# Out-projection of sixteen-head attention as three f16 products of split operands, on one Trainium2 core

## The reference

```python
q = jnp.einsum('bsd,hde->bhse', x, Wq)      # likewise k, v
scores = jnp.einsum('bhse,bhte->bhst', q, k)  # causal, / sqrt(64)
attn = jax.nn.softmax(scores, axis=-1)
out = jnp.einsum('bhst,bhte->bhse', attn, v)
heads = out.transpose(0, 2, 1, 3).reshape(B, S, H * E)
y = x + heads @ Wo                          # the out-projection
```

## Time and profile before

| | us |
|---|---|
| runs, median (lowest to highest of 3) | 846.56 (846.43 to 847.8) |
| the profiled execution, whole time | 846.91 |
| its span in the trace | 845.0 |
| busy: TensorE / its weight loads | 736.2 / 527.8 |
| busy: VectorE / ScalarE / GpSimd | 629.1 / 561.1 / 516.2 |
| output projection L890, 64 pairs, matmuls busy | 68.4 |
| idle of GpSimd ahead of L1022, until VectorE's split | 203.3 |

### The profile page before, as it was taken

The page is one execution under the profiler, slowest core; times in us unless marked ns, Lnnn a source line. Parts: engine busy times, 40 slices in busy tenths (PEclk is TensorE's granted clock), DMA queues, the critical chain, the costliest instruction groups (busy, mean ns, idle before and its releaser), DMA issues. The chain is left out here.

```text
span 845.0 us, 20974 instructions
## 1 busy us (share of the span) xinstructions
PE 736.2 (87%) x7594; PEld 527.8 (62%) x7594; DVE 629.1 (74%) x1291; ACT 561.1 (66%) x1551; POOL 516.2 (61%) x496
## 2 busy tenths in 40 slices
PE   4887678636999999999999999999999999999752
PEld 3656566533667766766676667667767667676541
DVE  1577766653766688689879877997898699789963
ACT  1466656633767766777777777777777777776633
POOL 3566653531655677666857775785667568666821
PEclk9998888778999999999999999999999999999965
DMA  7500000000798887877778878977787877788720
GB/s 189 127 1 1 0 2 0 1 0 18 146 152 142 146 146 140 145 143 137 144 139 149 148 143 138 153 139 147 141 142 141 145 146 143 151 139 157 136 50 23
DMA packets 360614, 94.00 MB, mean 111 GB/s; under 512 B 347584, under 2 KB 360384, under 8 KB 360512
## 3 DMA queue, kind: packets, MB, share of 16 engines
q1 hardware_dynamic: 357248, 90.57, 59.3%
q10 hardware_dynamic: 3264, 2.10, 0.8%
HBM read 6.63 MB, written 2.10 MB: 10 GB/s over the span
## 5 line engine op out<-in xcount | busy, mean ns | idle before, releaser
L1022 POOL TENSOR_TENSOR prob_hl<-prob,prob_hl 128x768 f16<-128x768 f32 (+1 forms) x192 | 347.4, 1809 | 203.3 <-DVE prob_hl L962 203.1
L933 ACT ACTIVATE prob<-wide,neg_max 128x128 f32<-128x128 f32 (+3 forms) x512 | 264.1, 524 | 157.7 <-DVE neg_max L974 157.6
L974 DVE TENSOR_REDUCE neg_max<-wide 128x2 f32<-128x256 f32 (+3 forms) x256 | 204.6, 820 | 111.7 <-PE wide L851 110.8
L846 PE MATMUL wide<-k_sb,q_sb 64*128 64x128 f32 (+3 forms) x1024 | 190.1, 469 | 0.9 <-ACT k_sb L828 0.8
L962 DVE CAST prob_hl<-prob 128x768 f16<-128x768 f32 (+1 forms) x192 | 155.0, 807 | 0.6 <-ACT prob L933 0.5
L871 PE MATMUL bank<-v_hi,prob_t 128*128 128x64 f16 x1280 | 133.1, 194 | 13.8 <-DMA prob_t<-prob_hl 12.2
L873 PE MATMUL bank<-v_hi,prob_t 128*128 128x64 f16 x1280 | 133.2, 194 | 0.0
L872 PE MATMUL bank<-v_lo,prob_t 128*128 128x64 f16 x1280 | 133.1, 193 | 0.0
L871 PEld LDWEIGHTS bank<-v_hi,prob_t 128*128 128x128 f16 x1280 | 115.8, 98 | 20.6 <-issue 13.7
L873 PEld LDWEIGHTS bank<-v_hi,prob_t 128*128 128x128 f16 x1280 | 114.5, 98 | 0.0
L872 PEld LDWEIGHTS bank<-v_lo,prob_t 128*128 128x128 f16 x1280 | 114.4, 98 | 0.0
(11 more groups left out here) (169 smaller groups left out, 1329.7 us busy)
## 6 DMA issues: line engine op xcount, KB each, us to landing
prob_t<-prob_hl SPq DMA_TRANSPOSE x384, 2.8
x_sb<-in_L_attn_a_in_features SPq DMA_DIRECT2D x8, 256.0 KB, 6.0
out_x<-x_done SPq DMA_DIRECT2D x8, 256.0 KB, 2.5
wq_a<-in_L_attn_a_w_q ACTq DMA_DIRECT2D x1, 512.0 KB, 5.2
wk_a<-in_L_attn_a_w_k ACTq DMA_DIRECT2D x1, 512.0 KB, 6.8
wo_a<-in_L_attn_a_w_o ACTq DMA_DIRECT2D x1, 512.0 KB, 7.5
wv_a<-in_L_attn_a_w_v ACTq DMA_DIRECT2D x1, 512.0 KB, 8.1
wq_b<-in_L_attn_b_Wq SPq DMA_DIRECT2D x1, 512.0 KB, 9.7
```

What stands on the lines that cost most here:

```text
L846: pe.matmul(dst[:, h, c:c + m], q[e, i * P:(i + 1) * P], k[e, 0:m], start=(i == UNIT_ROWS[u][0]), stop=False)
L933: last = act.activation(prob_2[s][:, at:at + m], score_banks(p, s)[:, h, c:c + m], ACT.Exp, bias=neg_max[p % 2][:, h, i:i + 1], accum_out= ...
L974: last = dve.tensor_reduce(neg_max[p % 2][:, :, i:i + 1], score_banks(p, s)[:, :, c:c + m], AX.X, ALU.max, negate=True)
L1022: pool.tensor_tensor(prob_hl[u][:, w:2 * w], prob_2[u][:, 0:w], prob_hl[u][:, 0:w], ALU.subtract)\
```

## The change

The weights Wo are divided by their own mean maximum and split into `wo_hi` and `wo_lo`, both f16, where they were multiplied by the scale of Wv before and stayed f32. ScalarE copies the turned context out of PSUM twice, to f16 (`ctx_t_hi`) and to f32 (`ctx_t`), and GpSimd subtracts one from the other in SBUF (`ctx_t_lo`, f16). It does so behind the low half of unit 1, in stage 1 of its own loop. The out-projection is three f16 products for each block where it was one f32 product, and waits for `ctx_t_lo`. The product of both scales is applied when YA is added to the residual.

```diff
...
         wv_b_lo = sb("wv_b_lo", [P, O], F32R)
-        wo_up = sb("wo_up", [P, HP, P])
-        largest = sb("largest", [P, 1])
+        wo_hi = sb("wo_hi", [P, HP, P], F16)
+        wo_lo = sb("wo_lo", [P, HP, P], F16)
+        y_scale = sb("y_scale", [P, 1])
+        largest = sb("largest", [P, 2])
         mean_of_rows = sb("mean_of_rows", [P, P])
-        scale_up = sb("scale_up", [P, 1])
-        scale_down = sb("scale_down", [P, 1])
+        scale_up = sb("scale_up", [P, 2])
+        scale_down = sb("scale_down", [P, 2])
...
         ctx_t = sb("ctx_t", [P, S])
+        ctx_t_hi = sb("ctx_t_hi", [P, S], F16)
+        ctx_t_lo = sb("ctx_t_lo", [P, S], F16)
         ffn_s = sb("ffn_s", [P, S])
...
         def scale_tensor(pe):
-            pe.wait_ge(sem("largest"), 1)
+            pe.wait_ge(sem("largest"), 2)
             pe.wait_ge(sem("mean_of_rows"), 1)
             pe.wait_ge(sem("at_g"), B)
-            pe.matmul(GX[:, 0:1], mean_of_rows[:, :], largest[:, :], start=True, stop=True).then_inc(sem("scale_ps"), 1)
+            pe.matmul(GX[:, 0:2], mean_of_rows[:, :], largest[:, :], start=True, stop=True).then_inc(sem("scale_ps"), 1)
...
                 .then_inc(sem("largest"), 1)
+            dve.tensor_reduce(largest[:, 1:2], wo_b[:, :, :], AX.XY, ALU.max, apply_absolute_value=True)\
+                .then_inc(sem("largest"), 1)
...
             act.copy(wv_b_hi[:, :], wv_b[:, :, :]).then_inc(sem("wv_b_hi"), 1)
+            act.wait_ge(sem("wo_b_scaled"), 1)
+            act.copy(wo_hi[:, :, :], wo_b[:, :, :]).then_inc(sem("wo_hi"), 1)
...
             dve.wait_ge(sem("scale_ps"), 1)
-            dve.tensor_scalar_max(scale_up[:, :], GX[:, 0:1], TINY).then_inc(sem("scale_up"), 1)
+            dve.tensor_scalar_max(scale_up[:, :], GX[:, 0:2], TINY).then_inc(sem("scale_up"), 1)
             dve.wait_ge(sem("scale_up"), 1)
...
                 .then_inc(sem("wv_b_scaled"), 1)
-            dve.tensor_scalar(wo_up[:, :, :], wo_b[:, :, :], scale_up[:, 0:1], None, ALU.mult)\
-                .then_inc(sem("wo_up"), 1)
+            dve.tensor_scalar(wo_b[:, :, :], wo_b[:, :, :], scale_down[:, 1:2], None, ALU.mult)\
+                .then_inc(sem("wo_b_scaled"), 1)
+            dve.tensor_tensor(y_scale[:, :], scale_up[:, 0:1], scale_up[:, 1:2], ALU.mult).then_inc(sem("y_scale"), 1)
...
                               ALU.subtract).then_inc(sem("wv_b_lo"), 1)
+            dve.wait_ge(sem("wo_hi"), 1)
+            dve.wait_ge(sem("wo_b_scaled"), 1)
+            dve.tensor_tensor(wo_lo[:, :, :], wo_b[:, :, :], wo_hi[:, :, :], ALU.subtract).then_inc(sem("wo_parts"), 1)
...
             n = number(b, p)
-            wait(pe, "ctx_t", n + 1)
+            wait(pe, "ctx_t_lo", n + 1)
             if p == 0:
...
             for i in range(QB):
-                last = pe.matmul(YA[:, i * P:(i + 1) * P], ctx_t[:, i * P:(i + 1) * P], wo_up[:, p, :],
-                                 start=(p == 0 and i == 0), stop=(p == HP - 1 and i == QB - 1))
+                block = slice(i * P, (i + 1) * P)
+                pe.matmul(YA[:, block], ctx_t_hi[:, block], wo_hi[:, p, :], start=(p == 0 and i == 0), stop=False)
+                pe.matmul(YA[:, block], ctx_t_hi[:, block], wo_lo[:, p, :], start=False, stop=False)
+                last = pe.matmul(YA[:, block], ctx_t_lo[:, block], wo_hi[:, p, :], start=False,
+                                 stop=(p == HP - 1 and i == QB - 1))
             last.then_inc(sem("y_ps"), 1)
...
                     wait(act, "y_ps", n - 2)
+                    wait(act, "ctx_t_lo", n - 2)
+                    act.copy(ctx_t_hi[:, :], MB[:, :]).then_inc(sem("ctx_t_hi"), 1)
                     act.copy(ctx_t[:, :], MB[:, :]).then_inc(sem("ctx_t"), 1)
...
             n = number(b, p)
+
+            def context_lower(u):
+                if u == 1 and pair_exists(*earlier(b, p, 2)):
+                    wait(pool, "ctx_t_hi", n - 1)
+                    wait(pool, "ctx_t", n - 1)
+                    wait(pool, "y_ps", n - 2)
+                    pool.tensor_tensor(ctx_t_lo[:, :], ctx_t[:, :], ctx_t_hi[:, :], ALU.subtract)\
+                        .then_inc(sem("ctx_t_lo"), 1)
+
             if pair_exists(b, p):
...
                         .then_inc(sem(f"pl{u}"), 1)
+                    context_lower(u)
                     back_gpsimd(pool, b, p, u)
...
                 for u in range(NU):
+                    context_lower(u)
                     back_gpsimd(pool, b, p, u)
...
                     m = 2 * len(unit_blocks(u))
-                    sp.wait_ge(sem("wo_up"), 1)
+                    sp.wait_ge(sem("wo_parts"), 1)
                     wait(sp, f"ph{u}", n + 1)
...
                     sp.dma_start_transpose(prob_t[u][:, 0:m, :], prob_hl[u][:, 0:m * P]).then_inc(sem(f"pt_hi{u}"), 16)
-                    sp.wait_ge(sem("wo_up"), 1)
+                    sp.wait_ge(sem("wo_parts"), 1)
                     wait(sp, f"pl{u}", n + 1)
...
             tokens = y_res[:, seq(c), :]
-            dve.tensor_tensor(tokens, YA[:, :].rearrange("p (a d) -> p a d", d=P), tokens, ALU.add)\
+            wait(dve, "y_scale", 1)
+            dve.scalar_tensor_tensor(out=tokens, in0=YA[:, :].rearrange("p (a d) -> p a d", d=P),
+                                     scalar=y_scale[:, 0:1], in1=tokens, op0=ALU.mult, op1=ALU.add)\
                 .then_inc(sem("y_acc"), 1)
...
             pe.wait_ge(sem("wqk_lo"), 2)
-            pe.wait_ge(sem("wo_up"), 1)
+            pe.wait_ge(sem("wo_parts"), 1)
             pe.wait_ge(sem("bn_xt_lo"), B)
...
```

## The result

The changed kernel takes 908.79 us (median, 907.77 to 913.11) against 846.88 before: a ratio of 1.074, 95% interval 1.070 to 1.078. Its profiled execution took 907.77 us with a span of 906.0. The forecast was 895 within 862 to 922, slower. The times of the experiments are medians of four to nine runs, of two in e2, e3 and e4.

What follows compares the result with a forecast made beforehand. TensorE, hardly waiting in the heads, was taken to bound the kernel before. The profiled 846.9 us plus 46 for the new loop, 2 for preparation and 0.5 at the end gave 895.4, forecast as 895 us, range 862 to 922.

Steps and rivals of the forecast that it cites:

- The loop: Heads: projection, scores, VectorE's maximum and split, GpSimd's low half, subtraction, next projection; plain pair 9.56 us, 46 us more in all.
- TensorE's products: Output projection: twelve f16 products at 0.058 us, 0.69 us for 0.98, saving 0.29 us per pair, 18.6 us in all.
- rival (a): Heads: GpSimd's subtraction is hidden and only TensorE's saving shows, 831 us; chance 0.06.
- The subtraction, 1.16 us: GpSimd, behind the low half of unit 1: 1.16 us per pair for 128 x 512, 74 us in all.
- Pair 3's loop: Projection to projection in pair 3 of a batch, with VectorE also centring or scaling: 10.83 us.
- pair 7's: Last pair of a batch, set by TensorE alone: 10.08 less 0.29, 9.8 us.
- rival (e): Heads: TensorE's waits lower the granted clock to 0.88, 41 us more, 936 us; chance 0.07.
- Pairs by batch: Heads, a batch of eight pairs: 81.0 us where it was 75.31.
- the same 61 steps: From first projection (229.80) to last (798.84), 569.0 us before: 614.8, and 0.9 for the first wait, 46.7 us more.
- ScalarE's copy, nothing: One more PSUM copy per pair, 0.47 us of ScalarE's queue, 30 us in all; counted as nothing.
- GpSimd's work apart from its place: VectorE's split and GpSimd do not run at once; loop 0.55 us later, up to 15 us, counted for upper end alone.
- Preparation 2, end 0.5: Ahead of the heads, second maximum, subtraction and cast: 2 us; after the last pair, exposed copy and subtraction: 0.5 us.

Runs made afterwards that it cites:

- e2: Changed kernel, but the third product reads the high half, so TensorE does not wait for the subtraction, which is still made; 870.45 us, ratio 1.029.
- e3: Changed kernel with GpSimd's subtraction made a second time, into a spare tile, ahead of the one that counts; 1022.77 us, ratio 1.209.
- e4: Kernel before, with its f32 projection, to which only the f16 copy, GpSimd's subtraction and the projection's wait are added; 930.52 us, ratio 1.100.
- e5: Changed kernel with GpSimd's subtraction moved ahead of the low half of unit 1; 870.76 us, ratio 1.027.
- e1: Changed kernel without the f32 copy, subtraction and its wait; the third product reads the high half again; 846.18 us, ratio 0.999.
- e9: e1 with one f16 product per block in place of three, leaving out the weights' low half too; 839.42 us, ratio 0.991.
- e11: Changed kernel with 24 products of a zero tile ahead of the projection's wait, for pairs 1 to 3 of a batch only; 901.35 us, ratio 1.065.
- e8: e1 with ScalarE's second copy added back, read by nobody, which the projection and value product wait for; 846.18 us, ratio 0.999.
- e10: Changed kernel with the subtraction made by VectorE straight from PSUM, no f32 copy on ScalarE and nothing added on GpSimd; 856.00 us, ratio 1.010.
- e7: Changed kernel with 24 or 12 products of a zero tile ahead of the projection's wait, in all pairs but a batch's first; 912.93 us, ratio 1.077.

## Why the prediction was right, point by point

- **The loop, and that the sign follows from it: right.** Plain pairs were given 9.56 us and took 9.55. So close a match has some luck in it: from one projection to the end of the low half (252.47 to 260.84) it was 8.37 us, given 8.31, and from there to the next projection 1.17, given 1.25. e5, which moves one line, takes 38 of the 62 us back, and e4 shows the loop without any f16 product.
- **TensorE's products: right in spacing, wrong in worth.** They stand 0.057 us apart, where 0.058 was taken, and not the 81 ns that the Trainium skill gives (TensorE: Matmul & The Clock Gate, Back-to-back issue gap). To the start of the next product the projection fell from 0.98 to 0.78 us: 0.20 saved, not 0.29, for the f32 product behind the last f16 one comes 0.15 us after it. Behind a wait the f32 projection takes 1.06 us (e4), and from e4 to the changed kernel it is 0.38 us per loop. But the text read TensorE's 74.61 of 75.30 us as "an edit that shortens its work would pay", and rival (a) priced that at 831 us. e1 is (a) made real, and takes 846. What failed is that reading: the record of busy matmuls covered slack (pair 4, above), and pairs 3 to 6 have another bound as long as TensorE's work. In pair 5 that is VectorE, busy for 9.40 of 9.40 us in e1; in the others e9's waits point to its chain. It did little harm to the sum, since inside the loop the saving counts.
- **The subtraction, 1.16 us: right** (median 1.167) where VectorE is not in between, and 1.60 where its split goes first. The prediction kept that case for the upper end of the range; it is the rule in steps 3, 4 and 6 of most batches. Pair 3's loop was given 10.83 and took 11.2; pair 7's was given 9.8 and took 9.56.
- **The clock, rival (e): partly true.** It was given 0.88 throughout or nothing. It came as short dips behind the longest waits, worth 7 us by e11. This is the term that the sum missed most by.
- **Pairs by batch:** 81.0 us forecast, 83.9 measured in the batch of the earlier trace rows (526.61 to 610.54), 81.6 in e11, without the dips. Over the same 61 steps it was 628.2 us (233.36 to 861.52) against 614.8 minus 0.7, so 14 more than the sum had; between the same points e11, where the dips are all but gone, has 9 us less over the last 56 of them. The last batch took 85.4 us where 80.3 was given: without a value product its pairs were short for TensorE alone, and that the loop takes no notice of.
- **ScalarE's copy, nothing: right** (e8). **GpSimd's work apart from its place: missed.** The text had named that VectorE's casts and GpSimd take turns, and priced only what that does to the subtraction. e2 shows 24 us of it with no wait at all. In the changed kernel the adds are hardly held (46.5 us in all, 70.7 in e2); it seems that the engines catch up while TensorE stands. So the forecast's sum did not need them, but a forecast of e5 would have.
- **Preparation 2, end 0.5:** the start measured 2.7 us more, clock included. The projection at 798.84, taken for the last, is the last but two; from it to the end it was 46.2 us before and 44.5 in the changed kernel, 1.7 less where 0.5 more was given. As expected, the very last projection stood 1.3 us for its subtraction. But in these drains the clock was at 1.2 GHz for most of the time in both kernels and at different places, so what the change itself costs there stays open. These misses and the 14 us above add up, to within 0.2 us, to the 12.4 us between the forecast's 895.4 and the 907.77 of the profiled execution.

## What to carry to other kernels

When work is moved to an idle engine, look at the place in that engine's order, not at its busy share: from the wait of the consumer back through each engine to the consumer again, that loop must be shorter than the period. Then ask of the work itself whom it holds up on the way, even if nobody waits for its result. And an engine that is recorded as busy for 99% may have a second engine right behind it; where it has, shortening the first gains nothing until that one is shortened too.

## What the runs showed of the hardware

- GpSimd and VectorE take turns in their use of SBUF, both ways: a VectorE add of two SBUF operands takes 0.74 us (its median before) and 1.61 behind a running GpSimd instruction (e2), a GpSimd subtraction 1.16 alone and 1.60 behind VectorE's cast. The Trainium skill (GPSIMD Engine Reference, Specifications) says that GpSimd's SBUF interfaces are shared with VectorE, with contention for instructions of two SBUF inputs or in a two-port mode; the trace agrees. VectorE's 64 subtractions of one PSUM and one SBUF operand in e10 took 0.68 to 0.69 us, though GpSimd was at work beside 62 of them.
- TensorE's granted clock fell to 1.2 GHz for short stretches (3.4 us, eight of them from 400 to 840 us) behind some of the waits of 2.2 to 2.6 us in a stream that was otherwise busy, and did not where products of zeros by the weights filled the waits (e7, e11).
- f16 products of 128 columns with 128 x 128 weights reloaded for each stand 0.057 us apart in a stream of twelve, f32 passes of the same shape 0.11 us (eight, each recorded with 0.275 us, within 1.05 us).
